# First attention of a six-layer kernel: weighted sums in three passes on high and low parts instead of two plain fp32 matmuls, with half of the next query projection in front of the first of them

## What is computed

```python
q = (x @ w_q)...; k = (x @ w_k)...; v = (x @ w_v)...
lq = x @ w_lq
lk = (lq @ w_lk)...
lv = (x @ w_lv)...
q = _apply_rope(q, cos, sin)
k = _apply_rope(k, cos, sin)
lk = _apply_rope(lk, cos, sin)
k = jnp.repeat(k, GROUPS, axis=1)
v = jnp.repeat(v, GROUPS, axis=1)
attn = _causal_attn(q, k, v, SCALE)
lat = _causal_attn(q, lk, lv, SCALE)
return attn @ w_o + lat @ w_lo
```

## Time and profile before

| | us |
|---|---|
| median of three runs | 1891.56 |
| the profiled execution | 1892.9 |
| its span | 1891.1 |
| the first attention, from 132 to 1399 us of the span | 1267 |
| TensorE busy in the whole span | 1765.6 |

### The profile page before, as it was taken

How to read it: one execution, slowest core, us unless ns; L and a number is a source line. 1 busy time by engine, 2 the same in 40 slices (tenths; PEclk the granted TensorE clock), 3 DMA queues, 4 the chain that set the end, 5 groups by cost and what they waited for, 6 DMA issues and landing times.

```text
span 1891.1 us, 34627 instructions
## 1 busy us (share of the span) xinstructions
PE 1765.6 (93%) x11076; PEld 1530.7 (81%) x11076; DVE 1124.1 (59%) x3334; ACT 1086.6 (57%) x3071; POOL 906.7 (48%) x1153
## 2 busy tenths in 40 slices
PE   7979999999999999999999999999989788898788
PEld 5769988988998898898899989899968566666566
DVE  5655565556546546545655654664566767677656
ACT  3336565566547556556655655664642445777854
POOL 4445544555545455444555445454423326668720
PEclk9989999999999999999999999999989998999999
DMA  3300021012002101101200110110011200000001
GB/s 124 111 23 18 7 64 39 1 36 68 7 18 59 33 1 57 53 1 35 62 13 18 57 36 1 46 62 1 29 56 28 90 31 20 2 1 24 18 7 45
DMA packets 35462, 66.19 MB, mean 35 GB/s; under 512 B 4032, under 2 KB 4672, under 8 KB 35264
## 3 DMA queue, kind: packets, MB, share of 16 engines
q1 hardware_dynamic: 35264, 63.73, 11.0%
HBM read 61.62 MB, written 2.10 MB: 34 GB/s over the span
## 4 chain that ended last, share of the span: by engine, by line
PE 69%; DVE 9%; issue 8%; ACT 8%; POOL 5%; DMA 0%; DVEq 0%; SPq 0%; ACTq 0%; POOLq 0%
PE bank L357 54%; PE bank L974 5%; PE bank L961 4%; PE bank L976 3%; ACT s L1079 2%; POOL s L1795 1%; PE bank L1510 1%; PE bank L1481 1%; PE bank L1497 1%; DVE h L676 1%; POOL WF L269 1%; ACT s L1566 1%; ACT W L256 1%; POOL W L269 1%; POOL rstd L322 1%
## 5 line engine op out<-in xcount | busy, mean ns | idle before, releaser
L357 PE MATMUL bank<-W,oT 128*128 128x512 f32 x1632 | 433.2, 402 | 1.0 <-DVE oT L1747 1.0
L1286 POOL TENSOR_TENSOR qk<-work,qk 128x512 fp32r<-128x512 f32 (+1 forms) x160 | 191.5, 1197 | 469.0 <-ACT qk L1070 469.0
L357 PEld LDWEIGHTS bank<-W,oT 128*128 128x128 f32 x1632 | 290.3, 190 | 49.3 <-issue 1.3
L1086 ACT COPY pt<-bank 128x384 f32<-128x384 f32 x256 | 122.0, 477 | 338.8 <-PE bank L961 338.5
L1278 POOL TENSOR_TENSOR work<-work,table 128x512 f32<-128x512 f32 (+1 forms) x160 | 192.1, 1201 | 139.2 <-ACT work L1065 139.2
L1079 ACT ACTIVATE s<-s,neg_max 128x128 f32<-128x128 f32 (+1 forms) x512 | 227.7, 446 | 49.5 <-DVE neg_max L1193 48.7
L357 PE MATMUL bank<-W,xnA 128*128 128x320 f32 (+1 forms) x1056 | 186.5, 333 | 3.1 <-DVE xnA L342 2.8
L357 PEld LDWEIGHTS bank<-W,xnA 128*128 128x128 f32 x1056 | 166.9, 188 | 16.6 <-DVE xnA L342 4.0
L1170 DVE TENSOR_TENSOR work<-bank,table 128x512 f32<-128x512 f32 (+1 forms) x160 | 101.9, 637 | 128.7 <-ACT work L1065 128.7
L357 PE MATMUL bank<-xnA,W 128*128 128x256 f32 (+1 forms) x1080 | 162.7, 301 | 8.0 <-DVE W L262 6.6
L357 PE MATMUL bank<-xnB,W 128*128 128x256 f32 (+1 forms) x1080 | 165.9, 304 | 3.3 <-DVE xnB L342 3.3
(11 more groups left out here) (106 smaller groups left out, 3516.7 us busy)
## 6 DMA issues: line engine op xcount, KB each, us to landing
raw<-in_weights SPq DMA_DIRECT2D x215, 256.0 KB, 2.8
x<-in_x SPq DMA_DIRECT2D x8, 256.0 KB, 5.9
out<-x SPq DMA_DIRECT2D x8, 256.0 KB, 2.1
row<-in_bias_rows SPq DMA_DIRECT2D x5, 256.0 KB, 2.7
table<-in_constants SPq DMA_DIRECT2D x4, 240.0 KB, 3.6
b_qk<-in_bias_rows SPq DMA_DIRECT2D x1, 512.0 KB, 3.8
b_val<-in_bias_rows SPq DMA_DIRECT2D x1, 256.0 KB, 3.0
table<-in_constants SPq DMA_DIRECT2D x1, 66.0 KB, 2.3
```

The costliest lines, as they stand in the source:

```text
L357: last = nc.tensor.matmul(out_ap, lhs(i), rhs(j), start=start and k == 0, stop=stop and k == 2)
L1086: nc.scalar.copy(pt0[:, k, :], bank[PT][:, 0:3 * P]).then_inc(a_pt, 1)
L1286: nc.gpsimd.tensor_tensor(lo, work[:, 2 + s, st.columns(what)], hi.bitcast(F32), ALU.subtract).then_inc(a_rope_lo, 1)
```

## The change

The tiles `lvv` and `pt0` become pairs of a high and a low part in F32R. Each weighted sum becomes two calls of `product`: three matmuls of 256 columns and three of 128. ScalarE's copy out of bank 4 now writes the high part of `pt0`, and a new VectorE subtraction of 128x384 (`turned_lo`) writes the low part; only that one counts `a_pt`. For the values ScalarE makes a new copy of 128x320 (`values_hi`), and VectorE's copy becomes a subtraction that waits for it. TensorE projects the first six of the twelve query matmuls before the first weighted sum, and the rest in the old place. A tile that only the lead uses (`normed`) shares its memory with `oT0`.

```diff
-                lvv = sb(s, "lvv", [P, 2, LVW])
-                pt0 = sb(s, "pt0", [P, 2, 3 * P])
+                lvv = [sb(s, f"lvv{i}", [P, 2, LVW], F32R) for i in (HI, LO)]
+                pt0 = [sb(s, f"pt0_{i}", [P, 2, 3 * P], F32R) for i in (HI, LO)]
...
-        def a0_queries(pe, st):
-
-            dst, to = a0_claim(pe, st, "q"), st.near(2)
-            for c in range(KC):
+        def a0_queries(pe, st, part=None):
+
+            to = st.near(2)
+            if part != 1:
+                a0_claim(pe, st, "q")
+            dst = bank[st.fill("q")[1]]
+            for c in range(KC) if part is None else range(2 * part, 2 * part + 2):
...
+            if part == 0:
+                return
...
-                nc.tensor.matmul(bank[OB][:, 0:SEQ], lvv[:, 0, col:col + P], pt0[:, k, 0:2 * P],
-                                 start=True, stop=False)
-                nc.tensor.matmul(bank[OB][:, P:SEQ], lvv[:, 1, col:col + P], pt0[:, k, 2 * P:3 * P],
-                                 start=False, stop=True).then_inc(a_pv, 1)
+                product(bank[OB][:, 0:SEQ], lambda p: lvv[p][:, 0, col:col + P],
+                        lambda p: pt0[p][:, k, 0:2 * P], True, False)
+                product(bank[OB][:, P:SEQ], lambda p: lvv[p][:, 1, col:col + P],
+                        lambda p: pt0[p][:, k, 2 * P:3 * P], False, True).then_inc(a_pv, 1)
...
+            if st.queries and not st.first:
+                a0_queries(pe, st, 0)
             if lag1:
                 weigh(0)
                 turn(1)
             if st.queries and not st.first:
-                a0_queries(pe, st)
+                a0_queries(pe, st, 1)
...
-                nc.scalar.copy(pt0[:, k, :], bank[PT][:, 0:3 * P]).then_inc(a_pt, 1)
+                nc.scalar.copy(pt0[HI][:, k, :], bank[PT][:, 0:3 * P]).then_inc(a_pt_hi, 1)
+
+            def values_hi(i):
+                tt, half = divmod(i, 2)
+                f, fs = st.fill(i)
+                act.wait_ge(a_proj, f + 1)
+                nc.scalar.copy(lvv[HI][:, tt, half * HALF:(half + 1) * HALF],
+                               bank[fs][:, 0:HALF]).then_inc(a_val_hi, 1)
...
             if lagging(st):
                 result_hi(1)
+            if st.h == 0 and st.heads:
+                for i in range(1 if st.first else 0, 4):
+                    values_hi(i)
...
+            def turned_lo(k):
+                n, _ = before.inst(k)
+                dve.wait_ge(a_pt_hi, n + 1)
+                nc.vector.tensor_tensor(pt0[LO][:, k, :], bank[PT][:, 0:3 * P],
+                                        pt0[HI][:, k, :].bitcast(F32), ALU.subtract).then_inc(a_pt, 1)
+
             def values(i):
...
-                nc.vector.tensor_copy(lvv[:, tt, half * HALF:(half + 1) * HALF],
-                                      bank[fs][:, 0:HALF]).then_inc(a_proj_free, 1)
+                nc.vector.tensor_tensor(lvv[LO][:, tt, cols], bank[fs][:, 0:HALF],
+                                        lvv[HI][:, tt, cols].bitcast(F32),
+                                        ALU.subtract).then_inc(a_proj_free, 1)
...
             if before.queries:
                 a0_rotate(dve, before, "q")
+            if lagging(st):
+                turned_lo(0)
             if st.heads:
                 minima(0)
                 minima(1)
...
             if lagging(st):
                 result_lo(0)
+                turned_lo(1)
```

More of the change, by code:

```diff
@@ L171, in program @@
                 qk = [sb(s, f"qk{i}", [P, 6, SEQ], F32R) for i in (HI, LO)]
-                lvv = sb(s, "lvv", [P, 2, LVW])
-                pt0 = sb(s, "pt0", [P, 2, 3 * P])
-                oT0 = [sb(s, f"oT0_{i}", [P, 4, SEQ], F32R) for i in (HI, LO)]
+                lvv = [sb(s, f"lvv{i}", [P, 2, LVW], F32R) for i in (HI, LO)]
+                pt0 = [sb(s, f"pt0_{i}", [P, 2, 3 * P], F32R) for i in (HI, LO)]
                 lqT = [sb(s, f"lqT{i}", [P, TOKENS], F32R) for i in (HI, LO)]
                 s0 = sb(s, "s0", [P, 4, 3 * P])
-                normed = sb(s, "normed", [P, 4, DIM])
+                with ExitStack() as entry:
+                    normed = sb(entry, "normed", [P, 4, DIM])
+                oT0 = [sb(s, f"oT0_{i}", [P, 4, SEQ], F32R) for i in (HI, LO)]
             with ExitStack() as s:
@@ L775, in program @@
         a_turned = sem("a_turned")
+        a_pt_hi = sem("a_pt_hi")
         a_pt = sem("a_pt")
+        a_val_hi = sem("a_val_hi")
         a_pv = sem("a_pv")
@@ L1101, in a0_scalar_step @@
                 a0_swap(act, st, "k")
+            if st.first:
+                values_hi(0)
             if st.heads:
@@ L1211, in values @@
                 f, fs = st.fill(i)
-                dve.wait_ge(a_proj, f + 1)
-                nc.vector.tensor_copy(lvv[:, tt, half * HALF:(half + 1) * HALF],
-                                      bank[fs][:, 0:HALF]).then_inc(a_proj_free, 1)
+                cols = slice(half * HALF, (half + 1) * HALF)
+                dve.wait_ge(a_val_hi, st.g * (4 * BATCH) + (4 * st.batch + i + 1))
+                nc.vector.tensor_tensor(lvv[LO][:, tt, cols], bank[fs][:, 0:HALF],
+                                        lvv[HI][:, tt, cols].bitcast(F32),
+                                        ALU.subtract).then_inc(a_proj_free, 1)
             turn_of = None if st.last_group else st.g
@@ L1225, in a0_vector_step @@
                 a0_cosine(dve, st, "q")
+            if st.heads:
+                inverses(0)
+            if st.first:
                 values(0)
             if st.heads:
-                inverses(0)
                 inverses(1)
```

## The result

The changed kernel takes 1940.36 us (median of four runs, 1939.75 to 1945.34), the kernel before in the same comparison 1890.35 us (1888.97 to 1893.09). The profiled execution took 1939.86 us, 47.0 more than that of before.

What follows compares the result with a forecast made beforehand. TensorE's matmuls were taken to bound normal steps; waits and longer sums add 2.0 us per four steps, +64 us over 32 runs, to the profiled 1892.9: 1957, named as 1956 because that execution was 1.3 above the median; range 1932 to 1975.

Steps and rivals of the forecast that it cites:

- TensorE's own work, +4 us: Weighted sums on TensorE: 0.69 us each instead of 0.65, k = 0 sums about 0.64; +4 us over 128 steps.
- One sign: Narrow F32R passes on TensorE should start 0.11 us apart; 0.06 or 0.22 would show the other bounds.
- The subtractions: VectorE's new work: 0.56 us for a 128x384 subtraction (bounds 0.50 and 0.62), 0.49 at 320 columns.
- Where the wait stands: TensorE's weighted sums wait for VectorE's `pt0` subtraction in nearly every step, some 60 us in all; h = 3 minima unchanged.
- All of it before the second sum: The some 60 us of waits for VectorE's `pt0` subtraction all stand before each step's k = 1 sum.
- What a step gets longer by: Waits of 0.82, 0.67, 0.19, 0.19 us in h = 1, 2, 3, 0; with longer sums 2.0 per four steps, +64 us.
- 0.56 and about 0.17 until the minima can start: VectorE before the minima: `turned_lo(0)` takes 0.56 us plus about 0.17; minima 0.63 late in h = 1, 0.41 in h = 2.
- the 0.11 from the end of the subtraction to the load: Before the second sum: TensorE's weight load begins 0.11 us after VectorE's subtraction ends, its matmul another 0.11 later.
- The cover of the first low part: Six query matmuls moved before the first sum give it 0.7 us more time, the second none.
- a pass at double the price: Rival: narrow F32R passes cost 0.22 us each, some 2012 us, up to 2020; chance 0.10.
- hidden low parts: Rival: VectorE reaches `turned_lo(1)` earlier, so only the matmuls count; +4 us, 1896; chance 0.05.
- faster: Rival: narrow passes take 0.064 us, weight loads hide and low parts stay hidden; -25 us, 1867; chance 0.05.

Runs made afterwards that it cites:

- e8: Changed kernel with the three 128-column passes of each sum widened to 256 columns, same weights; 1945.34 us against 1940.36 for the changed kernel.
- e5: Changed kernel with second probabilities' copy and low part ahead of the second exponentials and inverse, in steps without keys; 1931.21 us.
- e10: Changed kernel with a low part of the probabilities for the first sum only; ScalarE's copy alone releases the second; ratio 1.016 to the kernel before.
- e4: Changed kernel with all query matmuls put back behind the first weighted sum; 1972.4 us, 32 more than the changed kernel.
- e1: Changed kernel's six passes and moved queries, all passes reading high parts, no low parts made; 1898.89 us against 1893.99 for the kernel before.
- e2: Changed kernel with low parts made and waited for, but each sum the two plain fp32 matmuls of before on high parts; 1934.82 us.

## Why the prediction was right, and where it was off

- *TensorE's own work, +4 us*: right. With the passes alone a step is 0.03 to 0.04 longer, some 5 us. The six loads of a sum span 0.68 us (722.19 to the next load at 722.87, 0.69 forecast), and the e8 kernel shows that the columns do not set the narrow pass; its loads stand 0.11 us apart. One sign was read too simply: the matmuls of the first two narrow passes start 0.06 apart, and only from there on 0.11. Behind the wide passes a load starts 0.11 us ahead of its matmul, and 0.06 from the second narrow pass on, so the short distance uses up a lead; the loads themselves keep their 0.11. The Trainium skill, "TensorE: Matmul & The Clock Gate", section "LDWEIGHTS (loading the stationary operand)", gives a load as its columns divided by 1.2 GHz, 107 ns for these 128, and the spacing of 0.109 to 0.111 us agrees. The 81 ns for a pair of 128 columns in its section "Back-to-back issue gap" does not hold for these 4-byte weights: by it, as an estimate, three narrow passes would take 0.24 us and the sum 0.60.
- *The subtractions*: right. 0.553 us at 384 columns for 0.56, 0.492 at 320 for 0.49. ScalarE's new copy lasted 0.427 for 0.41.
- *Where the wait stands*: right for the wait that sets the step, 65.6 us of the loader's idle time for "some 60", in nearly every step before the second sum; the minima of h = 3 are not delayed (1.74 us). "All of it before the second sum" was wrong in h = 1: there the first sum waits too, and starts 0.3 us late. It costs nothing more there, because the second sum's operand comes later still, but it is the 0.30 us that stay when the second low part is quicker (e5) or gone (e10). I had said that the moved queries give the first sum 0.7 us more, and had not set that against the end of `turned_lo(0)`, at 2.20 in my own chain.
- *What a step gets longer by*: the mechanism right, the size too large. Forecast was 2.0 us for a run of four, measured 1.2, which over 32 runs is 26 us too much. Two terms were mis-sized. The first is "0.56 and about 0.17 until the minima can start". The minima start 0.08 us *before* the recorded end of `turned_lo(0)` (708.54 + 0.55 = 709.09, and 709.01), as other VectorE instructions do, so they were late by 0.39 instead of 0.63 in h = 1, and by 0.14 instead of 0.41 in h = 2; ScalarE's second copy of `pt0` is late by the same. I had used this very overlap for the rotation, and took 0.17 where the next instruction is of another kind. That is 0.25 us in each of two steps. The second is the 0.11 from the end of the subtraction to the load, from a single wait in the trace of before: here it is 0.05 (712.21 + 0.56 = 712.77, and 712.82), and 722.14 to 722.19, 0.06 less in all four steps. Together 0.5 + 0.24 = 0.74 us a run of four, 24 us of the 26.
- *What offset it*: some 5 us in the steps at the change of a group, and 3 us outside the attention, neither of which I had a term for; that they stood against the 26 is luck. Without these 8 us the time would lie at 1932, the lower end of the range. 4 + 60 was forecast; 38 + 5 + 3 = 46 was measured.
- *The cover of the first low part*: the query matmuls that I costed at nothing do hide it in h = 3 and 0, and this is worth 32 us (e4). In h = 1 and at the change of a group a part of it sticks out.
- *The rivals*: a pass at double the price is excluded by the load spacing and by e1; hidden low parts by e2, which costs 41 us with the old matmuls; faster by both. How much the chain is to blame was settled by taking its parts away: the second low part alone costs 0.11 to 0.17 us in each step; in h = 1 another 0.39 comes when the values' split and the first low part meet in front of the minima, and goes with either.

## What to carry to other kernels

Splitting an operand into parts moves work from TensorE to the engines that prepare it, and here TensorE did not even gain, since a pass of 128 columns costs its weight load. Before trading a plain matmul for three passes, compare two plain instructions with three loads, and then count what the new subtraction adds to the chain that ends at the matmul, not what it adds to an engine with 40% idle time. Two additions that each fit into a gap of the chain need not fit together: here either of two was free and the pair cost 0.39 us. Cover for one new step can be bought by moving independent matmuls in front of its reader, but only for the reader that they stand in front of.

## What the runs showed of the hardware

- An F32R pass of 128 columns costs 0.11 us, nearly what one of 256 costs (0.12); giving three of them 256 columns made the second sum 0.02 to 0.04 us longer. Its loads stand 0.11 us apart, also where two of its matmuls start 0.06 apart.
- VectorE's next instruction starts about 0.08 us before the recorded end of the one ahead, also when it is of another kind and reads another bank.
- The weight load of the second sum follows the end of the subtraction that it waits for by 0.05 us (0.08 at the first sum of h = 1).
- A stage that nobody touched differed by 10 us between the profiled executions of two kernels: 427.5 against 437.6 us of TensorE's busy time for the same matmuls, at a granted clock of 0.96 and 0.94. A gain of a few us in another stage can't be read from the total then.
